# A convolution and mixture-of-experts block on one core: a new step order on all engines, with a row buffer of its own for the last pair

## The reference

```python
x = x + conv(_ln_c(x))            # _ln_c: normalise over the 128 channels of a pixel
#   conv(v): avg, mx = mean and max of v over the pixels of an image
#            wt = softmax of (mx @ w2.T + b2) - (avg @ w1.T + b1), 9 taps a channel
#                 (the softmax's axis has length 1 there)
#            depthwise 3x3 convolution of v with wt, + bias, + v
t = tokens(x)                     # 32768 rows of 128
t = t + ffn(_ln_t(t))             # _ln_t: normalise each row
#   ffn(v): logits = v @ Wg + bg; the best 2 of 8 experts; softmax of the two logits
#           sum over the two of weight * (gelu(v @ W1[e] + b1[e]) @ W2[e] + b2[e])
```

## Time and profile before

| | us |
|---|---|
| Median of 3 runs | 1646.42 |
| Lowest and highest | 1645.32, 1646.55 |
| The profiled execution: time | 1645.53 |
| The profiled execution: span | 1643.7 |
| PE busy | 1506.0 (92% of the span) |
| DVE busy | 1347.3 (82%) |
| ACT busy | 1070.7 (65%) |
| POOL busy | 989.9 (60%) |

### The profile page before, as it was taken

One profiled execution on the slowest core, in us unless ns is written; L12 is line 12 of the kernel. 1 busy time (PEld: TensorE's weight loads), 2 busy tenths in 40 slices (PEclk: granted clock), 3 DMA queues, 4 the chain that ended last, 5 costly groups with the idle time before them and its releaser, 6 DMA issues.

```text
span 1643.7 us, 45749 instructions
## 1 busy us (share of the span) xinstructions
PE 1506.0 (92%) x12254; PEld 1118.7 (68%) x12255; DVE 1347.3 (82%) x2727; ACT 1070.7 (65%) x2410; POOL 989.9 (60%) x1061
## 2 busy tenths in 40 slices
PE   5899999999999489999999999999999999999766
PEld 2454554545455329888888888888888888888654
DVE  3568888888888849889899898989989899998644
ACT  5577777777775317777777777777777777777400
POOL 1004554555555665777777777777777777777500
PEclk7999999999999559999999999999999999999976
DMA  4201212222121181111111111111111111110099
GB/s 132 77 29 63 78 63 70 64 70 75 55 78 39 42 158 49 43 40 43 45 44 40 39 40 41 44 43 39 45 46 39 45 41 45 44 43 8 27 401 391
DMA packets 61927, 115.80 MB, mean 70 GB/s; under 512 B 15278, under 2 KB 38986, under 8 KB 61879
## 3 DMA queue, kind: packets, MB, share of 16 engines
q1 hardware_dynamic: 37080, 62.29, 12.7%
q0 software_dynamic: 18176, 34.27, 6.7%
q10 hardware_dynamic: 6624, 18.69, 3.1%
HBM read 60.22 MB, written 58.61 MB: 72 GB/s over the span
## 4 chain that ended last, share of the span: by engine, by line
POOL 37%; issue 21%; DMA 5%; POOLq 2%; PE 1%; DVE 1%; SPq 0%; ACT 0%
POOL xn L472 14%; POOL token_out L484 13%; POOL yt L479 8%; DMA ye<-token_out 4%; POOL rows_by_pair L460 1%; PE psV L979 1%; POOLq L484 1%; DMA rows_by_pair<-rows,idx 0%; POOLq L478 0%; POOLq L480 0%; POOLq L482 0%; PE psT L784 0%; POOLq L470 0%; SPq L391 0%; DMA rt<-rows_by_pair 0%
## 5 line engine op out<-in xcount | busy, mean ns | idle before, releaser
L1294 DVE TENSOR_TENSOR gl<-g,gh 128x512 f16<-128x512 f32 x624 | 493.5, 829 | 90.2 <-ACT gh L684 84.5
L460 POOL DMA_INDIRECT rows_by_pair<-rows,idx x256 | 272.0, 1063 | 323.5 <-issue 200.1
L484 POOL DMA_INDIRECT token_out<-yt,rt x312 | 339.9, 1090 | 186.5 <-POOL yt L479 132.7
L799 PE MATMUL psV<-lp,diag 128*128 128x512 f32 x576 | 275.1, 610 | 18.5 <-ACT cv L568 17.6
L684 ACT ACTIVATE gh<-g 128x512 f16<-128x512 f32 x468 | 276.1, 624 | 17.3
L677 ACT ACTIVATE g<-psV 128x512 f32<-128x512 f32 x312 | 185.4, 598 | 132.2 <-PE psV L918 99.3
L677 ACT ACTIVATE g<-psT 128x512 f32<-128x512 f32 x312 | 183.1, 597 | 111.3 <-PE psT L918 77.6
L472 POOL TENSOR_SCALAR xn<-rt 128x128 f32<-128x128 f32 x312 | 239.6, 775 | 11.1 <-DMA rt<-rows_by_pair 7.5
L939 PE MATMUL psR<-wall,gh 128*128 x1248 | 223.9, 274 | 13.5 <-issue 8.1
L939 PE MATMUL psG<-wall,gh 128*128 x1248 | 223.0, 273 | 0.0
L940 PE MATMUL psG<-wall,gl 128*128 x1248 | 214.3, 219 | 0.0
(11 more groups left out here) (212 smaller groups left out, 2980.8 us busy)
## 6 DMA issues: line engine op xcount, KB each, us to landing
rt<-rows_by_pair SPq DMA_DIRECT2D x156, 133.0 KB, 2.1
xb<-in_x_dram SPq DMA_DIRECT2D x32, 512.0 KB, 3.5
ye<-token_out SPq DMA_DIRECT2D x32, 512.0 KB, 7.8
out_dram<-oe ACTq DMA_DIRECT2D x32, 512.0 KB, 8.4
token_out<-yt,rt POOLq DMA_INDIRECT x312, 2.3
rows_by_pair<-rows,idx POOLq DMA_INDIRECT x256, 2.4
stage<-in_L_ffn_W_dram SPq DMA_DIRECT2D x1, 2048.0 KB, 9.3
rows_by_pair<-pad_rows SPq DMA_DIRECT2D x15, 133.0 KB
```

Of the source, the lines that this page charges most:

```text
L460: gp.indirect_dma_start(rows_dram, bass.IndirectOffsetOnAxis(ap=idx[p][:, b:b + 1].bitcast(U32), axis=0), rows[p][:, b, :], None).then_inc ...
L484: gp.indirect_dma_start(y_dram, bass.IndirectOffsetOnAxis(ap=rt[r][:, b, ID:ID + 1].bitcast(U32), axis=0), yt[r][:, b, :], None, bounds_ch ...
L799: ins = te.matmul(psConv.rearrange("p (h w) -> p h w", w=WW), diag[k][:, m, :], lp[j][:, y:y + HH // 2, dx:dx + WW], start=(m == 0), stop= ...
L1294: v.tensor_tensor(gl[side][q][:, cols], g[side][:, cols], gh[side][q][:, cols], ALU.subtract).then_inc(lo_done, 1)
```

## The change

The instructions stay the same but for their order. In each step:

- PE: `variance(0, 0)` of the next pair moves to the step's end. `centre` of the second image stands between the two halves of the first image's convolution, `centre` of the next pair's first image ahead of the last half. The 36 products of the tap logits come in one piece at the end, not in four.
- ACT: `inv_std(0, 0)` comes ahead of `diagonals(0)`, `sum_up(0)` ahead of `take(0, 0)`, `square(1)` ahead of `take(0, 1)`; the sums of squares of the second image are cut in two pieces of four blocks around `inv_std(1, 1)`; `sum_up(1)` comes after them, and `take(1, 1)` at the end.
- DVE: two taps, not three, of the first window piece ahead of `norm(0)`; `number` and `weigh` directly behind `place` and ahead of `split_pooled`.
- The last steps (no stage 2): DVE makes the choices first, and PE's `ranks` comes ahead of `turn(1)`.
- The last pair has a third buffer `rows[2]`, `idx[2]` with semaphores of its own, so neither `keep` nor `number` waits for the scatter of the pair two before. POOL's loop runs one round less, and the last two pairs are written out.

```diff
+            def row_slot(self, stage):
+
+                return 2 if self.last(stage) else self.slot(stage)
...
             def keep(st_, k):
-                p = st_.slot(3)
-                if not st_.fixed or st_.turns(3) > 0:
+                p = st_.row_slot(3)
+                if not st_.fixed or (st_.turns(3) > 0 and not st_.last(3)):
                     act.wait_ge(rows_out[2 * p + k], 16 * NBLK * st_.turns(3))
...
+                if st_.on(2):
+                    conv(st_, 0, 0, 0, len(taps_pe[0]))
+                if st_.on(1):
+                    centre_both(st_, 1)
+                if st_.on(2):
+                    conv(st_, 0, 1, 0, len(taps_pe[0]))
+                elif st_.on(4):
+                    ranks(st_)
+                if st_.on(3):
+                    turn(st_, 1)
+                if st_.on(1):
+                    variance(st_, 1, 0)
+                if st_.on(2):
+                    conv(st_, 1, 0, 0, 2)
+                if st_.on(1):
+                    variance(st_, 1, 1)
+                if st_.on(2):
+                    conv(st_, 1, 0, 2, N_PE)
+                    if st_.on(4):
+                        ranks(st_)
+                if st_.next().on(1):
+                    centre_both(st_.next(), 0)
+                if st_.on(2):
+                    conv(st_, 1, 1, 0, N_PE)
...
+                if st_.on(1):
+                    tap_logits(st_)
+                if st_.next().on(1):
+                    variance(st_.next(), 0, 0)
...
+                if st_.on(1):
+                    inv_std(st_, 1, 0)
...
+                if st_.on(4):
+                    expose(st_)
+                if st_.on(3):
+                    token_squares(st_, 1, 0, NBLK // 2)
+                if st_.on(1):
+                    inv_std(st_, 1, 1)
+                if st_.on(2):
+                    take(st_, 1, 0)
+                if st_.on(3):
+                    token_squares(st_, 1, NBLK // 2, NBLK)
+                    token_std(st_, 1)
...
             def step(st_):
+                early = st_.on(4) and not st_.on(2)
+                if early:
+                    first_choice(st_)
+                    second_choice(st_)
                 if st_.on(3):
-                    window(st_, 3, 1, 0, 3)
+                    window(st_, 3, 1, 0, 2)
...
                 if st_.on(4):
                     place(st_)
+                    number(st_)
+                    weigh(st_)
                 if st_.on(1):
                     split_pooled(st_)
-                if st_.on(4):
-                    number(st_)
-                if st_.on(4):
-                    weigh(st_)
```

More of the change, by code:

```diff
@@ L196, in conv_moe_block @@
         rank_read, routed_ready = sem("rank_read"), sem("routed_ready")
-        rows_out = [sem(f"rows_out{j}") for j in range(4)]
+        rows_out = [sem(f"rows_out{j}") for j in range(6)]
         ch_tap, ch_win, ch4, chb = map(sem, ("dve_tap_logits", "dve_window", "dve_s4", "dve_b"))
@@ L248, in conv_moe_block @@
         cv = [sb(f"cv{k}", [P, PIX], held=phase_a) for k in range(2)]
-        rows = [sb(f"rows{p}", [P, NB2, RW], held=phase_a) for p in range(2)]
+        rows = [sb(f"rows{p}", [P, NB2, RW], held=phase_a) for p in range(3)]
         phase_a.close()
@@ L379, in _ @@
             sp.wait_ge(tab_in, 16)
-            for j in range(4):
-                sp.wait_ge(rows_out[j], 16 * NBLK * (NIMG // 4))
+            for j, turns in enumerate((NU // 2, NU // 2, NU // 2 - 1, NU // 2 - 1, 1, 1)):
+                sp.wait_ge(rows_out[j], 16 * NBLK * turns)
             sp.wait_ge(padded, 16 * (NPAIR + 1))
@@ new lines, in step @@
+                if st_.first:
+                    for n in range(2, 4):
+                        high_taps(n)
+                if st_.on(1):
+                    inv_std(st_, 0, 1)
+                if st_.on(2):
+                    diagonals(st_, 1)
+                if st_.first:
+                    for n in range(4, 6):
+                        high_taps(n)
+                    gate_bias()
+                if st_.on(1):
+                    sum_up(st_, 0)
+                if st_.on(2):
+                    take(st_, 0, 0)
@@ new lines, in step @@
+                if st_.first:
+                    high_w2(0, E // 2)
+                if st_.on(3):
+                    token_squares(st_, 0, 0, NBLK)
+                    token_std(st_, 0)
+                    keep(st_, 0)
+                if st_.on(1):
+                    square(st_, 1)
+                if st_.first:
+                    high_w2(E // 2, E - 2)
+                if st_.on(2):
+                    take(st_, 0, 1)
+                if st_.on(1):
+                    inv_std(st_, 1, 0)
@@ L643, in step @@
+                if st_.on(1):
+                    sum_up(st_, 1)
+                if st_.on(3):
+                    keep(st_, 1)
                 if st_.next().on(1):
                     square(st_.next(), 0)
+                if st_.on(2):
+                    take(st_, 1, 1)
                 if st_.on(1):
@@ new lines, in step @@
+                    variance(st_, 0, 0)
+                    for n in range(2, 4):
+                        turn_weights(n)
+                if st_.on(3):
+                    turn(st_, 0)
+                if st_.on(1):
+                    variance(st_, 0, 1)
+                if st_.first:
+                    for n in range(4, 6):
+                        turn_weights(n)
+                    gate_products()
+                if st_.on(2):
+                    conv(st_, 0, 0, 0, len(taps_pe[0]))
@@ L1193, in step @@
                 if st_.on(3):
[L1194 to L1195 removed]
+                    window(st_, 3, 1, 2, N_DVE)
+                if st_.on(4) and not early:
                     first_choice(st_)
```

194 lines of the change are left out of this document (72 added, 122 removed).

## The result

| | before | after |
|---|---|---|
| Median (lowest to highest), us, 4 runs each | 1646.49 (1645.32 to 1647.14) | 1619.12 (1617.74 to 1623.35) |
| Ratio, 95% interval | | 0.9836, 0.9819 to 0.9853 |
| Profiled execution: time, span | 1645.53, 1643.7 | 1617.97, 1616.2 |
| Softmax's last instruction, step 2 | 103.42 | 95.33 |
| The same, step 15 | 514.64 | 483.62 |

The changed kernel is faster by 27.4 us; 1622 in 1613 to 1636 was forecast. By the start of phase B it is 28.1 us ahead: steps 0 to 2 give 8.1 us (103.42 - 95.33), steps 3 to 15 give 22.9 (411.22 against 388.29), and the tail takes 2.9 back (97.30 against 100.23 us from the softmax of step 15 to the first tile product).

A forecast was written before the change was run, and what follows sets the result against it. No engine is full; waits bound the kernel as three engines hand a pair around. Steady steps 19.2 + first steps 5.0 - tail 0.4 = 23.8 us off the median 1646.42 gives 1622.6, stated as 1622, range 1613 to 1636.

The forecast's parts named there:

- The steady step: Phase A's full steps: 30.15 us instead of 31.63, a gain of 1.48 each, 19.2 us over 13 steps.
- The walk: One steady step followed through DVE, ACT and PE from trace durations, with t = 0 at DVE's windows; gives 30.15 us.
- The first norm's wait for `sd`: DVE's wait of 1.28 us at `norm(0)` in each steady step should vanish.
- The second norm's wait: DVE at `norm(1)` in each steady step still waits 1.1 us for `sd`.
- PE's wait for `take`: After the convolution's first half, 0.86 us a step, gone because the centring products stand there.
- The cover of `weigh` and of the logits in one piece: At the step's end, pooled parts are ready at 24.1 and PE wants them at 25.9, so the shift costs nothing.
- The first steps: Steps 0 to 2: the same waits fall, 1.5 us a step and a little more, 5 us; bounds 2 and 7.
- The tail: Last steps up to phase B: weight parts end 1.9 us later, net cost 0.4 us; bounds -1.3 and +1.9.
- POOL's chain alone: Lower bound of the tail's cost, -1.3 us: only POOL's earlier start of pair 14 counts.
- wait of ACT for `rows_out`: Rival of a moved wait: `keep(0)` waits 0.8 us each step for scattered rows, time 1633; chance 0.14.
- The loads: Rival: image loads land late for PE's centring, deciding from a landing of 5.9 us; 1662 us, chance 0.04.
- The clock: Rival: each steady step's first half falls to 1.2 GHz, 3.1 us a step, time 1662; chance 0.03.

The follow-up runs named there:

- e1: Changed kernel with the second image's two centring products on PE back behind the second half of the first convolution; 1638.13 us, ratio to before 0.9930 to 0.9971.
- e2: Changed kernel with PE's step end as before, tap logits in four pieces ahead of the centring products; 1647.75 us, ratio to before 0.9998 to 1.0023.
- e10: Changed kernel with the edits of e3 and e9 joined; 1618.37 us, ratio to before 0.9802 to 0.9875.
- e3: Changed kernel with the last steps ordered as before, own row buffer kept; 1611.28 us in one run.
- e8: Changed kernel with two squares ahead of `inv_std(1, 1)`, `sum_up(1)` directly behind `take(1, 0)`, last steps as before; 1611.79 us, ratio to before 0.9768 to 0.9823.
- e9: Changed kernel with PE's wait for the weight parts moved behind the first two tiles' transposes; 1619.40 us, ratio to before 0.9817 to 0.9859.
- e12: The kernel of e3 timed again, no new code; 1614.33 us, ratio to before 0.9800 to 0.9828.
- e4: Changed kernel with two row buffers as before, order kept; 1620.45 us in one run.
- e7: Changed kernel with two sums of squares ahead of `inv_std(1, 1)`, not four; 1620.71 us, ratio to before 0.9807 to 0.9862.
- e11: Changed kernel with last steps ordered as before and two row buffers, leaving only the new order of full steps; 1617.14 us in one run.
- e5: Kernel before with only the last pair's own row buffer added; 1641.06 us in one run.
- e6: Changed kernel with all eight sums of squares of the second image ahead of `inv_std(1, 1)`, not four; 1648.04 us, ratio to before 1.0002 to 1.0031.

## Why the prediction was right, point by point

**The steady step: right, a little small.** 1.76 us a step against 1.48. The walk was of the longer of the loop's two steps and meets it within 0.1 us at each of its points but one, DVE's windows, done 0.3 late. The shorter one, with a second norm wait of 0.37 instead of 0.8, was not in it. The first norm's wait for `sd` vanished; 0.31 us is left there, but behind DVE's own window (`<-DVE x`). The second norm's wait was forecast at 1.1, measured 0.4 to 0.8; that term was too large. PE's wait for `take` is gone, as e1 shows by its return.

**The cover of `weigh` and of the logits in one piece: right.** The PE wait for the pooled parts, 13.3 us in e2, is absent in after but for 0.2 us once.

**The first steps: mis-sized, 8.1 against 5.0, and outside the bounds of 2 to 7.** Part of it is the clock. Windows of PE, 30 to 50 us, of before, of after and of e10, in this order (busy, clock, DMA share, GB/s): before runs at 0.50 and 0.68, after at 0.79 and 1.00, e10 at 0.50 and 0.83.

```profile
30.00:40.00 10.00, 6.32 (x42) 0.50 0.00 0
40.00:50.00 10.00, 8.51 (x13) 0.68 0.62 209
```

```profile
30.00:40.00 10.00, 6.54 (x45) 0.79 0.00 0
40.00:50.00 10.00, 10.00 (x24) 1.00 0.63 212
```

```profile
30.00:40.00 10.00, 7.39 (x43) 0.50 0.00 0
40.00:50.00 10.00, 9.95 (x20) 0.83 0.63 212
```

e10, whose first steps are those of after, has its softmax of step 2 at 97.83. There the gain is 5.6 us, close to the 5.0: 1.4 in step 0, 2.5 in step 1, 1.7 in step 2, though its clock too is above before's. The other 2.5 us of after's profile come with the earlier rise of the granted clock, which the profiles of the changed kernels show in part: e3, e8, e9 and e12 have t2 at 95.8 to 96.5, e4, e7, e10 and e11 at 97.5 to 98.1. Whether the new order makes the early rise likelier is open: the kernel before and e5, the only ones with the old steady steps, have two profiles, both with the late one.

**The tail: mis-sized, 2.9 lost against 0.4 and outside the upper bound of 1.9, by two errors in one direction.** The forecast put the weight products 1.9 us later by the choices ahead of the windows; from the first copy on it is 51.15 - 49.44 = 1.7, and e4 shows that the own buffer frees nothing there. The first error is the step "Before, tiles began at some 611.7, when the first two were normalised". In twelve profiles, all but those of e9 and e10, PE's first tile product follows the last weight part by 1.53 to 1.57 us (611.94 - 610.40 in before), while POOL's first rows begin anything from 0.3 us (before) to 5.1 us (e1, e7) ahead of the parts' end. In before the rows would have let it begin only some 0.2 us sooner, if PE takes the 1.66 us behind the first rows that it takes in e10 (581.24 - 579.58), so the two chains could not be told apart there. (The forecast's own figures, 612.3 and 611.7, give 0.6, not 0.4.) So the 1.9 counted in full, not as 0.4, and the lower bound of -1.3, "POOL's chain alone", was no bound. The trace's releaser (`<-POOL xn` in both kernels) had misled me: PE waits there for several semaphores in turn, and for the weight parts among them. The second is step 16's first half, which the forecast left as it was before; in after it took 7.20 us and not 6.63, and the copy behind it came 1.2 us later. In e9, the same instructions up to there, it is short (8.52). Windows of 20 us from the softmax of step 15, of before, of after and of e9: granted clock 0.84, 0.80 and 0.86, and the copy comes 8.69, 9.88 and 8.52 us after that softmax.

```profile
514.64:534.64 20.00, 18.95 (x65) 0.84 0.14 48
```

```profile
483.60:503.60 20.00, 19.10 (x66) 0.80 0.15 49
```

```profile
483.90:503.90 20.00, 19.11 (x69) 0.86 0.15 49
```

Hence 1.7 + 1.2 = 2.9 lost, the measured number, against 0.4. The same 1.2 us hides what POOL won. Its gap ahead of pair 14, 1.58 us in the earlier trace rows, is gone (0.30), as forecast, but it started pair 13 1.2 us later (25.74 us after the softmax against 24.54), so pair 14 starts at 48.5 in both kernels; and the rows, forecast 1.3 us sooner, come 2.0 later (97.5 against 95.5).

**The sum**: 22.9 + 8.1 - 2.9 = 28.1 at phase B's start, forecast 19.2 + 5.0 - 0.4 = 23.8. The steady step gives 3.7 us of the difference, the first steps 3.1, the tail takes 2.5 back.

**The rivals.** No wait of ACT for `rows_out` stands in steps 3 to 15 of after, so `keep` finds its rows scattered. The loads land in 3.6 us by the median, 7.6 at most (forecast: trouble from 5.9 in each step); PE waits for none there. The clock is 1.00 in the steady windows with 1 us of PE waits a step. The rule that frequent short idles let the clock swing (the Trainium skill, page "TensorE: Matmul & The Clock Gate", section "A second HAM failure mode: psum-queue depth-cycling") has no case in after, nor in before with twice the waits. In e6, with one wait of 2.4 us a step, the clock did fall in four of steps 3 to 15. So in this kernel a wait somewhat longer than the ones forecast may bring this rival about; that the wait is the cause is likely, not shown. Its price was too low: it took `turn` at 1.0 us more, and step 16's `turn(0)`, wholly at half clock, takes 2.0 more (4.3 against 2.3).

```profile
DMA to landing us min/median/max: 3.1/3.6/7.6
```

**What the change leaves lying.** Its own last-step order costs 4.3 us with the own buffer (51.15 against 46.82) and undoes the buffer's 2.6. Taken back, it gives 1614.33 us (ratio 0.9800 to 0.9828 against after's 0.9819 to 0.9853, which overlap: a gain is likely, and not sure by the times alone; the 4.3 us stand in five profiles with the old order and the own buffer (46.8) against seven with the new order (51.1)).

## What to carry to other kernels

Where engines hand one item round in a ring, walk one steady step with the durations and ready times of the trace; independent work put where one engine waits for another's copy can be worth more than its wait (here 1.09 us a step for 0.86), and two such places need not add. Look separately at the steps where the ring is not full: an order that is right for the full step may be wrong there, and here it cost more than the buffer beside it could give. Before a releaser is taken as the bound, measure in two kernels the distance from each candidate to the start; the one that stays constant (here 1.53 to 1.57 us behind the weight parts) is the likely bound, and an edit that moves that wait alone (here e9) shows it.

## What the runs showed of the hardware

- The granted clock at the end of step 0 and in step 16 takes one of a few courses from execution to execution of the same instructions. With it step 1 comes out up to 2.4 us apart (28.1 to 30.4 us in the ten profiles that share its instructions) and step 16 up to 1.4 (copy at 8.5 to 9.9). This is likely a good part of the 5 to 7 us by which the times of one kernel spread; e3 and e12, the one kernel with two profiles, are 1.9 us apart, 1.4 of it by the first tile product.
- In e6 the clock fell from 1.00 in four of thirteen steps, behind a wait of PE of 2.4 us that stands in every step. With waits of 1 us it never fell in the steady steps of after or before.
- From the first tile product to the end of the span the same instructions took 1030.5 to 1035.6 us, in e3 and e5 the least, in e7 and e10 the most. Two parts of it stand in the traces. The first is the clock behind that product, here in the ten us from it on, in after (1032.3 us) and in e3 (1030.5):

```profile
583.85:593.85 10.00, 9.45 (x63) 0.66 0.43 110
```

```profile
578.95:588.95 10.00, 9.45 (x77) 0.82 0.45 120
```

The second is the pace of phase B's loop: from 700 to 1400 us PE stands 12.9 us in e10 and 12.3 in e7 ahead of the down products (`psR`), and 9.2 to 9.9 in the other twelve profiles. That is 0.4% of the stretch, in the same instructions. Why is open. The rows of e10 and of after:

```profile
L975 PE MATMUL psR<-wall,gh 128*128 x932 | 167.3, 274 | 12.9 <-issue 6.7 <-DVE gl L1329 0.2
```

```profile
L978 PE MATMUL psR<-wall,gh 128*128 x932 | 167.3, 274 | 9.2 <-issue 5.3 <-DVE gl L1333 0.2
```

- POOL's 128x128 multiply took 0.44 us by the median and up to 1.9 us while DVE's 128x512 weight parts ran beside it; POOL's spans are rough, and no run took the two apart. The row of e9's `xn`, 576 to 583 us (min, median, max in ns); in after the longest is 1474.

```profile
L485 POOL TENSOR_SCALAR xn<-rt x7: 442/448/1913, 576.1 to 582.6; 128x128 f32<-128x128 f32 x7
```
